# Turns, one-hots and positions placed elsewhere in a one-core mixer and mixture-of-experts kernel

## What is computed

```python
h = layernorm(x) * (1 + ca) + sa
x = x + ga * mixer(h)                 # shift, norm, keys and values, a scan over time, output product
h = layernorm(x) * (1 + cb) + sb
probs = softmax(h @ Wr); topw, topi = top_k(probs, 4)
shared = (silu(h @ Wsg) * (h @ Wsu)) @ Wsd * sigmoid(h @ Wse)
pos = (cumsum(one_hot(topi)) * one_hot(topi)).sum(-1) - 1      # slot of a token in its expert, 64 slots
ye = (silu(xe @ Wg) * (xe @ Wu)) @ Wd                          # per expert, xe gathered by slot
x = x + gb * (shared + scatter_add(ye * w))
```

## Time and profile before

| | us |
|---|---|
| median of 3 runs | 710.15 (709.39 to 710.7) |
| the profiled execution | 709.6 |
| its span, first to last instruction | 707.8 |
| PE busy | 668.3 (94% of the span) |
| DVE busy | 365.3 (52%) |
| ACT busy | 288.6 (41%) |
| POOL busy | 185.3 (26%) |

### The profile page before, as it was taken

How to read it: one execution, slowest core, us unless ns; L and a number is a source line. 1 busy time by engine, 2 the same in 40 slices (tenths; PEclk the granted TensorE clock), 3 DMA queues, 4 the chain that set the end, 5 groups by cost and what they waited for, 6 DMA issues and landing times.

```text
span 707.8 us, 8884 instructions
## 1 busy us (share of the span) xinstructions
PE 668.3 (94%) x3218; PEld 464.7 (66%) x3218; DVE 365.3 (52%) x702; ACT 288.6 (41%) x552; POOL 185.3 (26%) x174
## 2 busy tenths in 40 slices
PE   4899688999998899999999999999999999999997
PEld 3666455767676667888665665666666666668875
DVE  3778677678687886764224222122132243225755
ACT  3445775666657543322324333232232252323231
POOL 1254475645627200000022222222222222110000
PEclk9799888999999999999999999999999999999999
DMA  7770200000222006304788888787799887716311
GB/s 274 247 249 0 77 16 31 15 31 30 75 90 106 28 1 228 144 1 181 258 274 272 273 271 273 256 291 261 246 343 311 273 276 253 230 22 238 119 55 65
DMA packets 50295, 118.27 MB, mean 167 GB/s; under 512 B 6904, under 2 KB 11084, under 8 KB 50252
## 3 DMA queue, kind: packets, MB, share of 16 engines
q1 hardware_dynamic: 45388, 109.31, 43.3%
q0 software_dynamic: 4864, 8.40, 5.4%
HBM read 100.87 MB, written 18.91 MB: 169 GB/s over the span
## 4 chain that ended last, share of the span: by engine, by line
PE 59%; DVE 4%; ACT 2%; issue 2%; POOL 1%; DMA 0%; DVEq 0%; POOLq 0%; ACTq 0%
PE bank L1692 26%; PE bank L1704 12%; PE bank L1747 11%; PE bank L1764 6%; PE bank L1735 2%; ACT xsH L866 1%; PE bank L1795 1%; PE bank L1753 1%; DVE prod L1227 1%; DVE xres L1265 1%; POOL ho L640 1%; ACT ytmp L917 1%; POOL xres L648 1%; DVE prodL L1229 0%; DVE egu L1329 0%
## 5 line engine op out<-in xcount | busy, mean ns | idle before, releaser
L1692 PE MATMUL bank<-xsH,wguH 128*128 128x512 f32 x352 | 143.4, 407 | 1.4 <-DVE xsL L1219 1.0
L1692 PE MATMUL bank<-xsL,wguH 128*128 128x512 f32 x352 | 137.6, 391 | 0.0
L1692 PE MATMUL bank<-xsH,wguL 128*128 128x512 f32 x352 | 137.3, 390 | 0.0
L1227 DVE TENSOR_TENSOR prod<-bank,silu 128x512 f32<-128x512 f32 x38 | 26.2, 690 | 111.6 <-PE bank L1692 91.8
L1692 PEld LDWEIGHTS bank<-xsH,wguH 128*128 128x128 f32 x352 | 66.3, 188 | 26.1 <-issue 11.1
L1704 PE MATMUL bank<-wdH,prodH 128*128 128x512 f32 x176 | 73.5, 418 | 6.5 <-DVE prodL L1229 4.4
L1747 PE MATMUL bank<-egu,xeT 128*64 128x352 f32 x512 | 79.3, 462 | 0.0
L698 POOL DMA_INDIRECT expert_sums<-ye,slot_to x32 | 48.9, 1528 | 115.5 <-DMA expert_sums<-ye,slot_to 89.7
L880 ACT ACTIVATE prodH<-prod 128x512 fp32r<-128x512 f32 x38 | 24.0, 631 | 127.8 <-DVE prod L1227 127.8
L1692 PEld LDWEIGHTS bank<-xsL,wguH 128*128 128x128 f32 x352 | 66.1, 188 | 14.6
L1692 PEld LDWEIGHTS bank<-xsH,wguL 128*128 128x128 f32 x352 | 66.3, 188 | 12.8 <-issue 0.7
(11 more groups left out here) (220 smaller groups left out, 998.2 us busy)
## 6 DMA issues: line engine op xcount, KB each, us to landing
egu<-in_L_ffn_Wg_dram SPq DMA_DIRECT2D x32, 704.0 KB, 5.6
egu<-in_L_ffn_Wu_dram SPq DMA_DIRECT2D x32, 704.0 KB, 7.5
ed<-in_L_ffn_Wd_dram SPq DMA_DIRECT2D x32, 512.0 KB, 4.9
h2T<-in_L_wmod_dram SPq DMA_DIRECT2D x6, 1024.0 KB, 9.0
ed<-in_L_ffn_Wd_dram SPq DMA_DIRECT2D x32, 192.0 KB, 5.7
h_rows<-ho SPq DMA_DIRECT2D x16, 256.0 KB, 2.0
expert_sums<-ye SPq DMA_DIRECT2D x16, 256.0 KB, 8.8
out_dram<-xres SPq DMA_DIRECT2D x16, 256.0 KB, 2.1
```

The source lines that it names most:

```text
L1227: v.tensor_tensor(to[:, :], uB[:, :], silu[:, :], ALU.mult).then_inc(prod_ok, 1)
L1692: ins = mm.matmul(bk[:, :], l[f][:, w, c, :], r[:, c, :], start=(k == 0), stop=(k == 3 * C - 1))
```

## The change

No work is added or taken away by the code; two loads of ACT's function table go, because two uses of one function now follow each other. By place:

- PE, step 16 and step 20: the turns of `amid(t)` ahead of the down products of tile 0 (and the first of tile 1) instead of behind them. PE, steps 18 and 19: the turn behind the up half instead of between the halves.
- DVE, the same two steps 16 and 20: the two `down` ahead of `scale_rows`.
- DVE after step 21: `shifted_logits` of the last group ahead of `scale_rows(15)`, which it followed at three instructions' distance; ACT: `exps` of that group ahead of unit 3's first silu.
- DVE unit 3: `experts_ones` behind the second chunk's `gate_up` instead of the first's.
- PE unit 4: `positions` behind chunk 1 instead of chunk 0; DVE: `counts_picked` behind chunk 1 (and behind the split of the down weights), the sum `positions` behind chunk 2.

```diff
@@ ACT, units
                     for f in range(n):
-                        gate_only(p, g, f)
                         if u == EARLY and f == 0:
                             exps(EARLY)
+                        gate_only(p, g, f)
                         pair_stages(u, 2 * f)
@@ DVE, mixer steps
+                    if t >= NT and s == 2:
+                        down(0, g, 0)
+                        down(0, g, 1)
                     if t >= 7:
                         scale_rows(t - 7)
...
-                    if g >= 0 and s == 2:
+                    if 0 <= g and s == 2 and t < NT:
                         down(0, g, 0)
                         down(0, g, 1)
...
+                shifted_logits(EARLY)
                 scale_rows(NT - 1)
                 down(0, EARLY - 1, 2)
                 sigma_of(EARLY)
-                shifted_logits(EARLY)
                 down(0, EARLY - 1, 3)
@@ DVE, units
                         gate_up(p, g, f)
-                        if u == EARLY and f == 0:
+                        if u == EARLY and f == 1:
                             experts_ones()
...
                         if f == (1 if u == ROUTE else 0) and g == 0 and p:
                             lo_weights(p, n)
-                        if u == ROUTE and f == 0:
+                        if u == ROUTE and f == 1:
                             counts_picked()
-                        if u == ROUTE and f == 1:
+                        if u == ROUTE and f == 2:
                             positions()
@@ PE, mixer steps
+                    turns_first, turns_last = t >= NT and s == 2, t >= NT + 2 and s < 2
+                    if turns_first:
+                        for q in amid(t):
+                            turn(q)
                     if g >= 0:
                         early_piece(g, 2 * s)
...
-                    for q in amid(t):
+                    for q in () if turns_first or turns_last else amid(t):
                         turn(q)
...
                     if g >= 0:
                         early_piece(g, 2 * s + 1)
-                    for q in late(t):
+                    for q in (amid(t) if turns_last else []) + late(t):
                         turn(q)
```

## The result

The changed kernel takes 711.32 us (median of 20 runs, 709.88 to 713.55) beside 710.38 us for the kernel before (20 runs, 709.36 to 711.39): ratio 1.0015, 95% interval 1.0008 to 1.0022. That is slower by 0.94 us: clear of no change, since the interval lies above 1, but less than the 0.2%, 1.4 us, that the prediction took for the least it could tell. It is 0.72 us above the forecast of 710.6; 0.23 of that comes from the kernel before, which took 710.15 us in the three runs of the forecast and 710.38 in these 20. The profiled execution of the changed kernel took 712.27 us, span 710.5, the third slowest of its 20.

The account below looks back on a forecast made before the run. PE bounds the kernel, following DVE from 150 to 280 us. Mixer lead 1.95 us, 0.8 after unit 3, becomes 1.3 behind in unit 4, less 0.7 given back: +0.2 to +0.7, taken +0.45, median 710.6; range 708.8 to 712.3.

Parts of the forecast that it names:

- a lead from the mixer: Steps 16 to 20: reordered turns and downs bring PE's down product at 223.94 to 222.0, 1.95 us ahead.
- cut down by the store: Unit 3: top_experts waits for the store to land, starts at 236.1; PE's second up half is only 0.8 us ahead.
- given up in unit 4: Unit 4: PE waits some 2.4 us for the second low weights, saves 0.75, and leaves 1.3 us behind.
- The clock: New waits of some 2.5 us at step 20 and in unit 4 might lower the granted clock; forecast kept 1.00.
- Rival 2: The clock falls in unit 4's new wait, costing 1.65 us: 712.3; chance 0.11.
- the forecast of +0.45: Whole kernel: change of +0.2 to +0.7 us, taken as +0.45, giving a median of 710.6.
- unit 3's longer wait would hide it: Step 20: a low-clock stretch, costing about 1.65 us, would be hidden by PE's longer wait in unit 3.
- what DVE keeps of the lead: Unit 3: DVE's scale_rows(15), at 232.63 before, starts 0.8 us earlier, not 1.95.
- the ring: Steps 17 to 20 and scale_rows(15): DVE, ACT and POOL wait on one another at their own pace, 1.35 us ahead.
- The wait for prodL at the third pair's end: Late unit 4: PE's old 0.30 us wait at 274.82 goes, giving back 0.4 us with the restart.
- that for ACT's tile: Late unit 4: PE's old 0.27 us wait at 276.76 goes, giving back 0.3 us.
- half of 0.13: Rival 3: DVE gets no lead in unit 3, 0.8 us later, 711.4; chance 0.13, half beyond the bound for slower.

Follow-up runs that it names:

- e4: The changed kernel plus nine matmuls nobody reads in unit 4, ahead of chunk 1's gate half, in PE's wait for the second low weights: 710.81 us.
- e1: The changed kernel with positions, the picked counts and their sum back in their old place: 709.46 us, ratio 0.9991.
- e9: The kernel before with only shifted_logits ahead of scale_rows(15) and the exponential ahead of unit 3's first silu: 710.74 us, ratio 1.0007.
- e5: The kernel before with only PE's turns of steps 16, 18 to 20 and DVE's two downs placed as in the change: 708.57 us.
- e6: e2 with DVE's wait for the stores of rows moved from ahead of top_experts to ahead of unit 3's first product: 707.98 us, ratio 0.9972.
- e2: The changed kernel with the one-hots as well as positions, picked counts and their sum back in their old place: 709.28 us, ratio 0.9990.
- e3: The kernel before with only positions, counts_picked and their sum a chunk later: 712.42 us, ratio 1.0027.
- e11: e1 with DVE's wait for the stores of rows moved to ahead of unit 3's first product: 708.27 us, ratio 0.9969.
- e8: e3 plus nine matmuls nobody reads in PE's wait for unit 4's second low weights: 711.22 us, ratio 1.0012.

## Why the prediction came out as it did

The mechanism was as forecast: a lead from the mixer, cut down by the store, and given up in unit 4 because `positions` no longer covers the low weights. One term, the clock, was sized too small.

| step | forecast | changed kernel |
|---|---|---|
| `keys_values` starts | 187.56 | 187.41 |
| sum of `project(12)` on DVE | 199.75 | 199.49 |
| PE's wait for `ho`, step 20 | 2.5 | 2.48 |
| first down product of tile 2, 223.94 before | 222.0 | 222.33 |
| `top_experts`, held by the store | 236.1 | 236.32 |
| second up half of unit 3 | 238.95 | 239.21 |
| down product after the second prodL | 244.1 | 244.47 |
| second low weights end; PE waits | 258.4; 2.4 | 258.61; 2.33 |
| `positions` | 264.0 | 265.94 |
| third down tile of unit 4 | 277.2 | 279.27 |

- **Right: where the gain goes.** The lead does not outlive unit 4: late positions cost 1.35 us by the medians even with the clock held up (e4 against e1), and the exponential's move delays `scale_rows(15)` and with it the store (e9). In e4, whose profiled execution kept the clock at 1.00 at both places, the stretch from step 16's output product to the third down tile is 277.79 - 183.82 = 93.97 us, 0.39 more than before, where the forecast was 0.45. That is one execution each.
- **The step that failed: "The clock".** The prediction named 1.00 between 215 and 265 us as a condition, and the profile breaks it twice. Its text took waiting alone for the cause, which e9 doesn't bear out (below). Rival 2 priced the fall at 1.65 us and gave it a chance of 0.11, as though a kernel had the fall or not. It comes in part of the executions, so a share of the price belonged in the sum. By the ratios that share is 0.65 us, which makes the forecast of +0.45 one of +1.1, beside +0.94 measured; with the wait filled e4 gave 710.81. The overlapping intervals leave the size open, and part of this closeness is luck. The runs' mean granted clocks do not help: the ten runs of the changed kernel at 0.980 have a median of 710.79 and the other ten 711.83, but the kernel before, without such a wait in unit 4, splits the same way (709.89 for 13 runs at 0.980 or more, 710.63 for the other 22 of one set).
- **Wrong in the same step: "unit 3's longer wait would hide it".** At step 20 the low clock used up PE's wait ahead of tile 2's first down product (0.78 us at 222.39 in e4, none in the changed kernel), but unit 3's wait was 0.98 us with the fall and 0.97 without, so it took up nothing. From the turn of step 20 to the second up half the changed kernel needs 21.66 us and e4 239.43 - 218.22 = 21.21: 0.45 us is paid.
- **Mis-sized: what DVE keeps of the lead.** DVE's four low parts of rows took 4.51 us from 227.11, beside two sums of POOL (226.89 to 229.87); in the kernel before, and in e9, which keeps the old mixer, they took 3.43, beside one (229.07 to 230.35 in before). So `scale_rows(15)` came 0.57 us early (232.63 to 232.06) and not 0.8. The working took the ring for one that only shifts.
- **Given back: less.** The wait for prodL at the third pair's end is gone, as said; that for ACT's tile stayed at 0.20 us (0.17 in e4) where 0 was forecast.
- **Not foreseen: the size of the mixer's gain.** By medians e5 is 1.6 us faster; the two profiled executions differ by 0.84 (708.76 and 709.6). The rest is in how the executions of the kernel before spread, up to 711.67 in that set, and isn't explained by a trace here.
- **A small slip.** The chance of "slower", 0.19, is 0.015 more than the cases give (0.11 and half of 0.13).

## What to carry to other kernels

Before moving work, ask what it covers: `positions` had a wait of 0.75 us of its own and covered one of 2.4 us. When a wait of DVE is said to be for "issue" or for a late engine, list its other conditions and follow each back: the store, 2.18 us behind its issue in four kernels, held the routing, and moving that one wait past the routing gave another 1.3 us (e6 under e2). Price a new long PE wait twice, once for itself and once, in part of the executions, for the clock behind it. And compare two profiles by a stretch inside each, not by their times from the span's start.

## What was not expected of the hardware

- **The clock fell in one execution and not in another of like waits, and once without a wait.** After 2.33 us it fell in the changed kernel's unit 4, after 2.48 us in e3's it did not; at step 20, behind waits of 2.45 to 2.51 us, it fell in six of eight profiled executions and not in e4 and e11. In e9 it fell at about 202 us, where the profile shows PE without idle time since 190 us:

```profile
190.00:201.90 11.90, 11.90 (x62) 8.49 (x61) 5.92 (x9) 8.80 (x17) 2.06 (x2) 1.00 0.07 24
202.00:205.30 3.30, 3.30 (x8) 2.59 (x9) 3.16 (x8) 1.11 (x3) 2.17 (x3) 0.51 0.00 0
```

Just ahead PE did 16 router matmuls of 34 columns (from 198.19) and the output product's four on 64 rows (from 199.99); the kernel before has the same list there, and its profiled execution kept 1.00. So a wait of this length is neither enough for a fall nor needed for one; what decides it stays open. The Trainium skill, "TensorE: Matmul & The Clock Gate", Part 1, tells of a kernel whose count of slow matmuls at its start differs from run to run; the traces here show the like in the middle of a kernel.

- **One and the same subtraction took 0.69 or 1.53 us, by which engine came first.** In the kernel before POOL's sum begins at 184.87 and DVE's prodL 0.3 us behind it. DVE:

```profile
185.17 1.53 DVE L1229 TENSOR_TENSOR prodL<-silu,prodH 128x512 fp32r<-128x512 f32 x1 [1.14 <-ACT prodH L880]
```

POOL:

```profile
184.87 1.28 POOL L648 TENSOR_TENSOR xres<-xres,bc 128x512 f32<-128x512 f32 x1 [1.49 <-DMA bc<-vector_rows]
```

In e3, whose code is the same up to here, both begin at 184.70, DVE 5 ns ahead in the trace. DVE:

```profile
184.70 0.69 DVE L1229 TENSOR_TENSOR prodL<-silu,prodH 128x512 fp32r<-128x512 f32 x1 [1.16 <-ACT prodH L880]
```

POOL:

```profile
184.70 1.83 POOL L648 TENSOR_TENSOR xres<-xres,bc 128x512 f32<-128x512 f32 x1 [1.79 <-DMA bc<-vector_rows]
```

Here DVE is short and POOL long. PE's wait of 0.87 us for this prodL is missing in e3's execution, so a part of the gain read from one profile at step 16 hangs on who comes first; the other two profiled executions with the old order there, e8 and e9, have the wait (0.96 and 1.05 us). The Trainium skill, "SBUF — State Buffer", SBUF: two separate sides, says that DVE with two inputs in SBUF and a POOL instruction that reads SBUF contend for a pair of ports, and that the first to start keeps it for its whole instruction. These four rows agree.
